# Two of the 16 row-tile transposes of each channel pair go from TensorE to a DMA transpose of two f16 parts

## The chip, the cores and the metric

The kernel runs on one core of one Trainium2 chip. Its time is the device time of one execution in microseconds (us); lower is better. A TensorE column stream, VectorE, ScalarE, GpSimd and SyncE (which here only issues DMAs) run side by side and meet at semaphores.

## What is computed

A residual block over 64 sequences of 128 channels and 2048 positions: a mixing matrix chosen for each sequence, then for each channel a long convolution with a decaying kernel K (a sum of 64 complex exponentials), a direct term, and a mask by length.

```python
x = x + einsum('bct,bcd->bdt', x, weights[condition])           # 64 x 128 x 2048
K = 2 * einsum('hn,hnl->hl', Ct, exp(dtA[:, :, None] * arange(L))).real
y = irfft(rfft(x, 2L) * rfft(K, 2L))[..., :L] + x * D[:, None]   # causal convolution
x = x + y * (arange(L) < length[:, None])
```

## The kernel before, in words

The first part (some 320 us) multiplies each sequence by its matrix plus the identity and stores the result u to a DRAM scratch, channel by channel. Its instructions are L506, L680, L433 and the loads and stores around them. The change doesn't touch it.

The second part walks over 64 pairs of channels (h = 0 and 1 within a pair). The 2048 positions of a channel are cut into 8 pieces of 256; a row tile `u_row` holds 128 rows (2 x 64 sequences) and NG = 4 groups of 256 positions. For every pair:

- TensorE transposes the f32 row tile in 128x128 blocks (`transpose_u`, L518): 16 blocks, k = 0 to 15, where q = k // 4 is (channel, half of 128 positions) and g = k % 4 is the group. The four groups of a q fill one PSUM bank.
- ScalarE turns that bank into the high f16 part of `u_t` (`u_hi`, L694), and VectorE makes the low part, scaled bank less high part (`u_lo`, L958).
- `inputs_to_state` (L532, 12 matmuls of 448 columns) makes what each piece adds to the state, with the table `gt_sb`, which two DMA transposes make (L314).
- `advance` (L544, 6 small matmuls, j = 1 to 6) carries the state from piece to piece. Each j needs the state of the one before in f16: ScalarE `state_hi` (L702), then VectorE `state_lo` (L963).
- `out_part` (L567, L573, L576; k = 0 to 7) makes the outputs from `toep` (a Toeplitz table), `u_t`, `x_t` (a rearranged copy of part of `u_t`, `first_half`, L973) and the states. ScalarE empties the bank (`out_evac`, L710), VectorE lays the unmasked rows of `u_row` over it (`overlay`, L988), and SyncE stores it (L327).
- GpSimd makes the tables of later pairs: `outer` (L409 for the products g_x and g_y, two each, then L413), `outer_lo` (L418) and `make_lambda` (L425).

The order on each engine is written out by hand, slot by slot. In slot c TensorE does `out_part` k = 0, 1 of pair c-1, then `inputs_to_state` of pair c, then k = 2 to 7 of pair c-1 with `advance` 1 to 6 of pair c behind them. The transposes of pair c+1 are put into the `out_part`s, two in each (`between`). VectorE and ScalarE follow tables of steps: "s" state, "u" parts of u_t, "o" output, "t" `fold_toeplitz` (L980), "x" `first_half`, "g" g_hi. VectorE's table is

```python
steps = (("s", c - 1, 7), ("u", c, 3), ("o", c - 2, 3), ("t", c, 0), ("u", c + 1, 0),
         ("o", c - 1, 0), ("s", c, 1), ("x", c, 0), ("s", c, 2), ("x", c, 1), ("s", c, 3), ...
```

All loads, stores and DMA transposes of this part are issued by SyncE, in the order of its `slot`.

Of the kernel before, what the change touches and what calls it, by code (L numbers as in the profile page):

```python
# [38 lines left out]
LENGTHS = 8  # L39
WAVES = 5  # L40
XS = 6
STAGES = 4
# [23 lines left out]
def build(nc, x, cond, length, w_in, log_dt, c_in, log_a, a_im, d_in, out):  # L66
# [6 lines left out]
    with ctx:  # L73
# [15 lines left out]
        ident = sb("ident", [P, P], F32)  # L89
        eyes = sb("eyes", [P, 2, NM], F16)  # L90
        lam_v = sb("lam_v", [P, H, 2, 2], F16)
        mask_i = sb("mask_i", [P, Q], I32)
# [99 lines left out]
        s_gt = [sem(f"s_gt{i}") for i in range(2)]  # L192
        s_st, s_sth, s_stl = (sem(n) for n in ("s_st", "s_sth", "s_stl"))
        s_xt, s_tz = sem("s_xt"), sem("s_tz")
        s_out, s_y, s_ov = (sem(n) for n in ("s_out", "s_y", "s_ov"))
# [41 lines left out]
        def state(t, part, j):  # L237
            return ap(t, part * NG * ROWS + at(j), [[2 * NG * ROWS, 2], [1, NB]])

        def new_state(j):  # L240
# [10 lines left out]
        def _(sp):  # L251
# [59 lines left out]
            def transpose_g(i, c):  # L311

                for lo in (0, NM):
                    sp.dma_start(gt_sb[c % 2][:, :, :, :, lo:lo + NM].rearrange("p h a b m -> p (h a b) m"),  # L314
                                 g_sb[c % 4][NM - lo:P - lo, :, :, :].rearrange("p h a t -> p (h a t)"),
                                 transpose=True).then_inc(s_gt[c % 2], 16)

            def store_out(i, c, h):
                o = 2 * (c % 2) + h
                if (c, h) == (PAIRS - 1, 1):  # L320
                    for v in range(2):
                        store_last(sp, 0, v)
                    return
                sp.wait_ge(s_ov, 4 * (UN * i + c) + 2 * h + 2)
                for j in range(JJ):
                    dst = bass.AP(out.tensor, (2 * (UN * i + c) + h) * T + j * NG * Q, [[H * T, NB], [1, NG * Q]])
                    sp.dma_start(dst, o_sb[o][j * NB:(j + 1) * NB, :, :].rearrange("p g t -> p (g t)"))\  # L327
                        .then_inc(s_store[o], 16)
# [17 lines left out]
            def slot(i, c):  # L346
# [24 lines left out]
                if c == 0:  # L371
                    store_half(NB - 1, 1, EARLY, H, s_last)
                elif c < EARLY // 2 - 2:
                    for n in range(SPLIT_FROM + 2 * c - 2, SPLIT_FROM + 2 * c):
                        store_half(n, 1, EARLY, H, s_kept)
                if has(i, c - 1):
                    store_out(i, c - 1, 0)
# [93 lines left out]
        def _(pe):  # L471
# [38 lines left out]
            def transpose_u(i, c, k):  # L510

                q, g, n = k // NG, k % NG, UN * i + c
                if k % 8 == 0:
                    pe.wait_ge(s_row[c % 4][k // 8], 16 * (i + c // 4 + 1))
                if g == 0:
# [3 lines left out]
                                    u_row[c % 4][:, h, g, tb * P:(tb + 1) * P], ident[:, :])  # L519
                if g == NG - 1:  # L520
                    last.then_inc(s_ut, 1)
# [3 lines left out]
            def inputs_to_state(i, c):  # L525
                n = UN * i + c
                pe.wait_ge(s_gt[c % 2], 32 * (UN // 2 * i + c // 2 + 1))
                pe.wait_ge(s_ul, 4 * n + 4)
                wait(pe, s_stl, 7 * n)
                for h in range(2):  # L530
# [95 lines left out]
        def _(act):  # L626
# [62 lines left out]
            def u_hi(i, c, q):  # L689
                n = UN * i + c  # L690
                act.wait_ge(s_ut, 4 * n + q + 1)
                if q == 0:
                    wait(act, s_out, 4 * (n - 3))
                act.activation(u_t[c % 4][:, q // 2, q % 2, 0, :], bank[:, 4 + q, :], ACT.Copy, scale=US)\  # L694
                    .then_inc(s_uh, 1)

            def state_hi(i, c, j):
# [21 lines left out]
            def slot(i, c):  # L719
                steps = (("s", c - 1, 7), ("u", c, 3), ("o", c - 2, 3), ("g", c + 2, 0), ("u", c + 1, 0),  # L720
                         ("o", c - 1, 0), ("s", c, 1), ("s", c, 2), ("u", c + 1, 1), ("s", c, 3),
                         ("o", c - 1, 1), ("s", c, 4), ("s", c, 5), ("u", c + 1, 2),
                         ("s", c, 6), ("o", c - 1, 2))
                for what, of, k in steps if c else first:
# [5 lines left out]
                    if has(i, of):  # L730
                        if what == "s":
                            state_hi(i, of, k)
                        elif what == "u":
                            u_hi(i, of, k)
                        elif what == "o":
                            out_evac(i, of, k)
                        else:
                            g_hi(i, of)
# [6 lines left out]
        def _(dve):  # L745
# [209 lines left out]
            def u_lo(i, c, q):  # L955
                dve.wait_ge(s_uh, 4 * (UN * i + c) + q + 1)
                t = u_t[c % 4]
                dve.scalar_tensor_tensor(out=t[:, q // 2, q % 2, 1, :], in0=bank[:, 4 + q, :], scalar=US,  # L958
                                         in1=t[:, q // 2, q % 2, 0, :], op0=MUL, op1=SUB).then_inc(s_ul, 1)

# [5 lines left out]
            def first_half(i, c, part):  # L966

                n = UN * i + c
                if part == 0:
                    dve.wait_ge(s_ul, 4 * n + 4)  # L970
                    wait(dve, s_out, 4 * (n - 1))
                to = slice(NM, P) if part == 0 else slice(0, NM)
# [26 lines left out]
            def slot(i, c):  # L999
                steps = (("s", c - 1, 7), ("u", c, 3), ("o", c - 2, 3), ("t", c, 0), ("u", c + 1, 0),  # L1000
                         ("o", c - 1, 0), ("s", c, 1), ("x", c, 0), ("s", c, 2), ("x", c, 1), ("s", c, 3),
                         ("u", c + 1, 1), ("s", c, 4), ("o", c - 1, 1), ("s", c, 5), ("u", c + 1, 2), ("s", c, 6), ("o", c - 1, 2))
                for what, of, k in steps if c else first:
                    if has(i, of):
# [4 lines left out]
                        elif what == "u":  # L1009
                            u_lo(i, of, k)  # L1010
                        elif what == "x":
                            first_half(i, of, k)
# [28 lines left out]
```

## Time and profile before

| | |
|---|---|
| Time, median of 3 runs | 1087.58 us (1077.77 to 1088.26) |
| The profiled execution | 1079.03 us |
| Its span, first to last instruction | 1077.2 us |
| Mean granted TensorE clock | 0.996 |
| Busy: PE, DVE, ACT, POOL | 93%, 72%, 51%, 47% of the span |

The profile names engines PE (TensorE), PEld (its weight loads), DVE (VectorE), ACT (ScalarE), POOL (GpSimd), SP (SyncE; SPq is what it issues to its DMA queue). A row of the timeline is start, duration, engine, line, operation, output<-inputs, shapes, count; in square brackets the idle time ahead of it and who ended it. Matmul rows overlap, since the ends of matmuls are modelled: the distance from one start to the next is what an instruction costs the engine.

### The profile page before, as it was taken

The page shows a single profiled execution, that of the slowest core. Times are in us where ns is not written, and L with a number is a line of the kernel's source. Part 1 is how long each engine was busy: PE and PEld are TensorE (multiplying, and loading weights), DVE is VectorE, ACT ScalarE, POOL GpSimd, SP SyncE. Part 2 cuts the span into 40 slices and gives each one's busy share as a digit, 9 for nine tenths or more (in the row PEclk, how much of TensorE's full clock was granted, in tenths as well). Part 3 has the DMA queues.
Part 4 walks back from the last instruction along what each step waited for, and adds up shares of the span by engine and source line. Part 5 has one row for each costly group of instructions (what it writes and reads, how often), then busy time and mean ns, then how long its engine had stood idle before and what let it go on. Part 6 is the DMA issues. An engine that isn't in the chain of part 4 may idle for free.

```text
span 1077.2 us, 29210 instructions
## 1 busy us (share of the span) xinstructions
PE 1001.6 (93%) x11616; PEld 737.0 (68%) x11616; DVE 770.7 (72%) x1711; ACT 546.6 (51%) x1162; POOL 503.0 (47%) x542
## 2 busy tenths in 40 slices
PE   7977779677898999999999999999999999999998
PEld 4333234222347888888888888888788888888886
DVE  3988950000017888888888888888888888888885
ACT  2643434344444555556555555555555555555543
POOL 2211041200205666666655665665665665666630
PEclk9999999999999999999999999999999999999999
DMA  9999999999999999999999999999999999999994
GB/s 328 423 422 424 422 424 423 377 424 424 424 339 320 265 270 270 232 240 234 217 243 221 223 237 226 233 232 225 223 234 211 227 233 225 225 228 234 231 213 119
DMA packets 171719, 305.48 MB, mean 284 GB/s; under 512 B 80370, under 2 KB 113522, under 8 KB 163394
## 3 DMA queue, kind: packets, MB, share of 16 engines
q1 hardware_dynamic: 171266, 303.16, 99.5%
q8 instruction: 94, 1.54, 0.6%
q14 instruction: 39, 0.32, 0.1%
q0 software_dynamic: 160, 0.20, 0.1%
q10 hardware_dynamic: 160, 0.26, 0.1%
HBM read 152.37 MB, written 134.41 MB: 266 GB/s over the span
## 4 chain that ended last, share of the span: by engine, by line
PE 76%; DMA 17%; ACT 3%; issue 2%; SPq 1%; DVE 1%; ACTq 0%
PE bank L567 16%; DMA u_scratch<-stage 15%; PE bank L576 15%; PE bank L532 13%; PE bank L518 10%; PE bank L506 9%; PE bank L544 7%; PE bank L573 5%; ACT stage L680 2%; DMA x_f<-in_x 1%; DVE x_t L973 1%; DMA u_row<-u_scratch 1%; SPq L314 1%; ACT ring L680 0%; SPq L266 0%
## 5 line engine op out<-in xcount | busy, mean ns | idle before, releaser
L567 PE MATMUL bank<-toep,u_t 128*128 128x192 f16 (+1 forms) x3072 | 342.7, 220 | 0.1
L576 PE MATMUL bank<-g_sb,st_sb 128*128 128x256 f16 x1536 | 305.9, 273 | 0.4 <-issue 0.4
L506 PE MATMUL bank<-x_f,w_buf 128*128 128x512 f32 x512 | 236.7, 608 | 60.4 <-ACT stage L680 43.2
L518 PE MATMUL bank<-ident,u_row 128*128 128x128 f32 x1024 | 277.6, 275 | 2.2 <-issue 1.2
L702 ACT ACTIVATE st_sb<-bank 128x128 f16<-128x128 f32 x448 | 123.8, 276 | 287.8 <-PE bank L544 195.6
L567 PEld LDWEIGHTS bank<-toep,u_t 128*128 128x128 f16 x3072 | 231.4, 98 | 15.2 <-issue 1.4
L506 PEld LDWEIGHTS bank<-x_f,w_buf 128*128 128x128 f32 x512 | 93.8, 192 | 198.0 <-issue 109.7
L988 DVE COPY_PREDICATED o_sb<-mask,u_row 128x512 f32<-128x512 uint8 x256 | 206.1, 805 | 16.5 <-issue 16.5
L958 DVE SCALAR_TENSOR_TENSOR u_t<-bank,u_t 128x512 f16<-128x512 f32 x256 | 176.3, 689 | 37.5 <-ACT u_t L694 35.6
L573 PE MATMUL bank<-toep,x_t 128*128 128x64 f16 x2048 | 188.1, 193 | 0.5 <-issue 0.5
L425 POOL TENSOR_TENSOR lam_sb<-eyes,lam_v 128x512 f16<-128x512 f16 x64 | 75.5, 1180 | 231.7 <-PE bank L544 231.7
L694 ACT ACTIVATE u_t<-bank 128x512 f16<-128x512 f32 x256 | 152.2, 595 | 53.1 <-PE bank L518 48.6
L680 ACT ACTIVATE stage<-bank 128x1024 f32<-128x1024 f32 x100 | 96.8, 1021 | 150.7 <-DMA u_scratch<-stage 119.5
L963 DVE TENSOR_TENSOR st_sb<-bank,st_sb 128x128 f16<-128x128 f32 x448 | 129.8, 290 | 54.6 <-ACT st_sb L702 51.2
L573 PEld LDWEIGHTS bank<-toep,x_t 128*128 128x128 f16 x2048 | 157.5, 98 | 0.6 <-issue 0.6
L532 PE MATMUL bank<-u_t,gt_sb 128*128 128x448 f16 x768 | 155.7, 352 | 1.9 <-DMA gt_sb<-g_sb 1.9
L710 ACT ACTIVATE o_sb<-bank 128x512 f32<-128x512 f32 x256 | 153.3, 599 | 4.1 <-PE bank L576 4.0
L576 PEld LDWEIGHTS bank<-g_sb,st_sb 128*128 128x128 f16 x1536 | 149.3, 98 | 5.8
L518 PEld LDWEIGHTS bank<-ident,u_row 128*128 128x128 f32 x1024 | 143.8, 141 | 10.9 <-issue 1.5
L544 PE MATMUL bank<-st_sb,lam_sb 128*128 128x64 f16 x2304 | 130.1, 192 | 2.9 <-DVE st_sb L963 2.3
L433 POOL TENSOR_TENSOR w_buf<-w_f,ident 128x128 f32<-128x128 f32 x64 | 33.5, 528 | 210.3 <-PE bank L506 205.6
L409 POOL TENSOR_TENSOR g_y<-alpha_im,beta_im 128x256 f32<-128x256 f32 x128 | 129.8, 1033 | 0.0
(130 smaller groups left out, 880.3 us busy)
## 6 DMA issues: line engine op xcount, KB each, us to landing
x_f<-in_x SPq DMA_DIRECT2D x64, 1024.0 KB, 19.6
u_row<-u_scratch SPq DMA_DIRECT2D x128, 512.0 KB, 5.8
out<-o_sb SPq DMA_DIRECT2D x254, 256.0 KB, 3.8
u_scratch<-stage SPq DMA_DIRECT2D x50, 1024.0 KB, 17.7
toep<-k_scratch SPq DMA_DIRECT2D x64, 256.0 KB, 6.0
u_scratch<-ring SPq DMA_DIRECT2D x13, 512.0 KB, 14.6
u_scratch<-kept SPq DMA_DIRECT2D x10, 448.0 KB, 6.9
gt_sb<-g_sb SPq DMA_TRANSPOSE x128, 5.5
```

The lines of the kernel that those rows point to most:

```text
L409: pool.tensor_tensor(out=ap(dst[r], h * Q, [[16, 16], [1, 16]]), in0=ap(ta, o, [[1, 16], [0, 16]]), in1=ap(tb, o, [[0, 16], [1, 16]]), op= ...
L506: last = pe.matmul(bank[:, 4 * (n % 2) + k, :], w_buf[n % XS][:, :], x_f[n % XS][:, k * 512:(k + 1) * 512], start=True, stop=True)
L518: last = pe.transpose(bank[:, 4 + q, g * P:(g + 1) * P], u_row[c % 4][:, h, g, tb * P:(tb + 1) * P], ident[:, :])
L532: last = pe.matmul(bank[:, h, 0:(NJ - 1) * NB], gt_sb[c % 2][:, h, a, 1 - tb, :], u_t[c % 4][:, h, tb, b, 0:(NJ - 1) * NB], start=(m == 0) ...
L544: last = pe.matmul(bank[:, h, at(j):at(j) + NB], lam_sb[c % 2][:, h, a, :, :].rearrange("p k m -> p (k m)"), st_sb[c % 2][:, h, b, at(j):a ...
L567: pe.matmul(bank[:, y, col + tb * P + NM:col + Q], u[:, h, tb, a, rows_], t[:, h, b, NM:Q - tb * P], start=first, stop=False, skip_group_c ...
L573: pe.matmul(bank[:, y, col + tb * P:col + tb * P + NM], x_t[c % 2][:, h, tb, rows_], t[:, h, b, 0:NM], start=False, stop=False, skip_group ...
L576: last = pe.matmul(bank[:, y, col:col + Q], st[:, h, a, gr * ROWS:(gr + 1) * ROWS], g[:, h, b, :], start=False, stop=(m == 2), skip_group_ ...
L694: act.activation(u_t[c % 4][:, q // 2, q % 2, 0, :], bank[:, 4 + q, :], ACT.Copy, scale=US)\
L710: act.activation(o_sb[o][:, 2 * (v % 2):2 * (v % 2) + 2, :].rearrange("p g t -> p (g t)"), bank[:, 2 + v % 2, :], ACT.Copy, scale=1.0 / (U ...
L958: dve.scalar_tensor_tensor(out=t[:, q // 2, q % 2, 1, :], in0=bank[:, 4 + q, :], scalar=US, in1=t[:, q // 2, q % 2, 0, :], op0=MUL, op1=SU ...
L988: dve.copy_predicated(o_sb[2 * (c % 2) + v // 2][:, g2, :].rearrange("p g (b t) -> p (g b) t", t=P), mask[:, g2, :].rearrange("p g (b t) - ...
```

## The change

From the fourth pair on (`TURNED = 3`), for channel h = 0 of each pair (`TH = 1`), the last of the four groups of rows (g = 3) isn't transposed by TensorE. ScalarE makes the high f16 part of those 256 columns straight from the row tile (`parts_hi`), VectorE the low part (`parts_lo`), both into a new buffer `parts` with one copy, and one DMA transpose of 128 x 512 f16 elements writes both into `u_t` (`transpose_parts`). So TensorE does 14 transposes a pair in place of 16, over 61 pairs 122 less. `u_hi` and `u_lo` of q = 0 and 1 handle 384 columns in place of 512.

```diff
+        parts = sb("parts", [P, TH, 2, 2, P], F16)
+        def groups(c, h):
+            return NG - 1 if c >= TURNED and h < TH else NG
...
+            def transpose_parts(c):
+                sp.wait_ge(s_pl, c - TURNED + 1)
+                wait(sp, s_out, 4 * (c - 3))
+                sp.dma_start(ap(u_t[c % 4], (NG - 1) * ROWS, [[NG * ROWS, TH * 4], [1, ROWS]]),
+                             parts[:, :, :, :, :].rearrange("p h b a t -> p (h b a t)"), transpose=True)\
+                    .then_inc(s_pt, 16)
...
+                if TURNED <= c + 1 < PAIRS:
+                    transpose_parts(c + 1)
                 if has(i, c - 1):
                     store_out(i, c - 1, 0)
...
                 q, g, n = k // NG, k % NG, UN * i + c
+                if g >= groups(c, q // 2):
+                    return
...
                 pe.wait_ge(s_ul, 4 * n + 4)
+                wait(pe, s_pt, 16 * (n - TURNED + 1))
...
+            def parts_hi(c):
+                for h in range(TH):
+                    act.wait_ge(s_row[c % 4][h], 16 * (c // 4 + 1))
+                wait(act, s_pt, 16 * (c - TURNED))
+                act.activation(parts[:, :, :, 0, :],
+                               u_row[c % 4][:, 0:TH, NG - 1, :].rearrange("p h (b t) -> p h b t", t=P),
+                               ACT.Copy, scale=US).then_inc(s_ph, 1)
...
-                         ("o", c - 1, 0), ("s", c, 1), ("s", c, 2), ("u", c + 1, 1), ("s", c, 3),
+                         ("o", c - 1, 0), ("p", c + 1, 0), ("s", c, 1), ("s", c, 2), ("u", c + 1, 1), ("s", c, 3),
...
+                cols = groups(c, q // 2) * ROWS
+                dve.scalar_tensor_tensor(out=t[:, q // 2, q % 2, 1, 0:cols], in0=bank[:, 4 + q, 0:cols], scalar=US,
+                                         in1=t[:, q // 2, q % 2, 0, 0:cols], op0=MUL, op1=SUB).then_inc(s_ul, 1)
+            def parts_lo(c):
+                dve.wait_ge(s_ph, c - TURNED + 1)
+                dve.scalar_tensor_tensor(out=parts[:, :, :, 1, :],
+                                         in0=u_row[c % 4][:, 0:TH, NG - 1, :].rearrange("p h (b t) -> p h b t", t=P),
+                                         scalar=US, in1=parts[:, :, :, 0, :], op0=MUL, op1=SUB).then_inc(s_pl, 1)
...
                     dve.wait_ge(s_ul, 4 * n + 4)
+                    wait(dve, s_pt, 16 * (n - TURNED + 1))
...
-                         ("o", c - 1, 0), ("s", c, 1), ("x", c, 0), ("s", c, 2), ("x", c, 1), ("s", c, 3),
+                         ("o", c - 1, 0), ("p", c + 1, 0), ("s", c, 1), ("x", c, 0), ("s", c, 2), ("x", c, 1), ("s", c, 3),
```

On VectorE, in every slot, from `fold_toeplitz` to the second state. Before:

```order
L980 COPY toep<-toep 64x4x64 [waits s_t3]
L958 SCALAR_TENSOR_TENSOR u_t<-bank,u_t 128x512 [waits s_uh]
L986 MEMSET pad 1x1 [waits s_y]
L988 COPY_PREDICATED o_sb<-mask,u_row 128x512
L963 TENSOR_TENSOR st_sb<-bank,st_sb 128x2x64 [waits s_sth]
L973 COPY x_t<-u_t 64x2048 [waits s_out,s_ul]
L963 TENSOR_TENSOR st_sb<-bank,st_sb 128x2x64 [waits s_sth]
```

And in the changed kernel, where line numbers are larger:

```order
L1022 COPY toep<-toep 64x4x64 [waits s_t3]
L993 SCALAR_TENSOR_TENSOR u_t<-bank,u_t 128x384 [waits s_uh]
L1028 MEMSET pad 1x1 [waits s_y]
L1030 COPY_PREDICATED o_sb<-mask,u_row 128x512
L998 SCALAR_TENSOR_TENSOR parts<-u_row,parts 128x2x128 [waits s_ph]
L1004 TENSOR_TENSOR st_sb<-bank,st_sb 128x2x64 [waits s_sth]
L1015 COPY x_t<-u_t 64x2048 [waits s_out,s_pt,s_ul]
L1004 TENSOR_TENSOR st_sb<-bank,st_sb 128x2x64 [waits s_sth]
```

The new instruction stands between the overlay and the first state of the pair; the copy behind that state has a wait for the DMA transpose more.

On SyncE, one slot. Before:

```order
L314 DMA_TRANSPOSE gt_sb<-g_sb 128x8x64 [waits s_st,s_g]
L314 DMA_TRANSPOSE gt_sb<-g_sb 128x8x64
L327 DMA out<-o_sb 64x1024 [waits s_ov]
L327 DMA out<-o_sb 64x1024
L301 DMA u_row<-u_scratch 128x1024 [waits s_ov]
L308 DMA toep<-k_scratch 128x4x256 [waits s_out]
L327 DMA out<-o_sb 64x1024 [waits s_ov]
```

Changed:

```order
L323 DMA_TRANSPOSE gt_sb<-g_sb 128x8x64 [waits s_st,s_g]
L323 DMA_TRANSPOSE gt_sb<-g_sb 128x8x64
L343 DMA out<-o_sb 64x1024 [waits s_ov]
L343 DMA out<-o_sb 64x1024
L310 DMA u_row<-u_scratch 128x1024 [waits s_ov]
L317 DMA toep<-k_scratch 128x4x256 [waits s_out]
L330 DMA_TRANSPOSE u_t<-parts 128x4x128 [waits s_out,s_pl]
L343 DMA out<-o_sb 64x1024 [waits s_ov]
```

The new transpose is issued behind the `toep` load and ahead of the next output store.

## Rows read from the trace of the kernel before

**Rows 1.** Busy us of PE, PEld, DVE, ACT, POOL, then clock, DMA share, GB/s

```profile
700.00:800.00 100.00, 99.14 (x1464) 84.22 (x1462) 86.97 (x191) 55.98 (x140) 61.60 (x59) 1.00 1.04 228
```

**Rows 2.** Waits from 500 to 1000 us: total, times, longest

```profile
PE bank L544 <- DVE st_sb L963: 1.9, 4, 0.8
```

**Rows 3.** TensorE's timeline: transposes inside out_part, and one pair

```profile
706.94 0.27 PE L518 MATMUL bank<-ident,u_row 128*128 128x128 f32 x1
707.04 0.33 PE L567 MATMUL bank<-toep,u_t 128*128 128x192 f16 x2
...
707.85 2.43 PE L532 MATMUL bank<-u_t,gt_sb 128*128 128x448 f16 x12
...
711.17 0.34 PE L544 MATMUL bank<-st_sb,lam_sb 128*128 128x64 f16 x6
...
713.55 0.33 PE L544 MATMUL bank<-st_sb,lam_sb 128*128 128x64 f16 x6
...
719.47 2.43 PE L532 MATMUL bank<-u_t,gt_sb 128*128 128x448 f16 x12
```

**Rows 4.** VectorE's timeline in the same pair

```profile
707.39 0.73 DVE L988 COPY_PREDICATED o_sb<-mask,u_row 128x512 f32<-128x512 uint8 x1
...
708.15 1.03 DVE L980 COPY toep<-toep 64x256 f16<-64x256 f16 x1
709.22 0.69 DVE L958 SCALAR_TENSOR_TENSOR u_t<-bank,u_t 128x512 f16<-128x512 f32 x1
709.83 1.02 DVE L988 COPY_PREDICATED o_sb<-mask,u_row 128x512 f32<-128x512 uint8 x1
...
710.75 0.27 DVE L963 TENSOR_TENSOR st_sb<-bank,st_sb 128x128 f16<-128x128 f32 x1
711.05 0.80 DVE L973 COPY x_t<-u_t 64x2048 f16<-64x2048 f16 x1
711.88 0.29 DVE L963 TENSOR_TENSOR st_sb<-bank,st_sb 128x128 f16<-128x128 f32 x1
712.20 0.69 DVE L973 COPY x_t<-u_t 64x2048 f16<-64x2048 f16 x1
```

**Rows 5.** GpSimd's timeline in the same pair

```profile
707.82 1.28 POOL L418 TENSOR_TENSOR g_sb<-g_x,g_sb 128x512 f16<-128x512 f32 x1 [0.62 <-ACT g_sb L651]
709.07 1.19 POOL L409 TENSOR_TENSOR g_x<-alpha_re,beta_re 128x256 f32<-128x256 f32 x2
710.22 2.10 POOL L409 TENSOR_TENSOR g_y<-alpha_im,beta_im 128x256 f32<-128x256 f32 x2
712.41 1.62 POOL L413 TENSOR_TENSOR g_x<-g_x,g_y 128x512 f32<-128x512 f32 x1
```

**Rows 6.** VectorE in the last pair, when GpSimd has ended

```profile
1057.53 0.22 DVE L980 COPY toep<-toep 64x256 f16<-64x256 f16 x1
```

**Rows 7.** The pair from 765.32 us: VectorE, GpSimd, TensorE, and its window

```profile
769.91 1.80 DVE L973 COPY x_t<-u_t 64x2048 f16<-64x2048 f16 x1
...
769.88 1.28 POOL L413 TENSOR_TENSOR g_x<-g_x,g_y 128x512 f32<-128x512 f32 x1
...
772.18 0.34 PE L544 MATMUL bank<-st_sb,lam_sb 128*128 128x64 f16 x6 [0.76 <-DVE st_sb L963]
...
765.32:778.00 12.68, 11.82 (x170) 9.83 (x168) 11.22 (x23) 6.48 (x17) 7.03 (x8) 1.00 0.96 214
```

**Rows 8.** VectorE by line and shape (count, busy, mean ns); ScalarE's timeline

```profile
L755 DVE SCALAR_TENSOR_TENSOR ex<-ex 128x256 f32<-128x256 f32 x8 | 3.5, 443 | 0.3
...
710.32 0.28 ACT L702 ACTIVATE st_sb<-bank 128x128 f16<-128x128 f32 x1 [1.40 <-PE bank L532]
```

**Rows 9.** SyncE's queue in the pair, and transposes' issue to landing, 440 to 1050 us

```profile
711.85 0.43 SPq L308 DMA_DIRECT2D toep<-k_scratch  x1
715.21 1.12 SPq L327 DMA_DIRECT2D out<-o_sb  x2
...
DMA to landing us min/median/max: 3.2/5.5/7.9
```

More of the change, by code:

```diff
@@ L40 @@
 WAVES = 5
+TURNED = 3
+TH = 1
 XS = 6
@@ L193, in build @@
         s_st, s_sth, s_stl = (sem(n) for n in ("s_st", "s_sth", "s_stl"))
+        s_ph, s_pl, s_pt = (sem(n) for n in ("s_ph", "s_pl", "s_pt"))
         s_xt, s_tz = sem("s_xt"), sem("s_tz")
@@ L519, in transpose_u @@
                                     u_row[c % 4][:, h, g, tb * P:(tb + 1) * P], ident[:, :])
-                if g == NG - 1:
+                if g == groups(c, h) - 1:
                     last.then_inc(s_ut, 1)
@@ L693, in u_hi @@
                     wait(act, s_out, 4 * (n - 3))
-                act.activation(u_t[c % 4][:, q // 2, q % 2, 0, :], bank[:, 4 + q, :], ACT.Copy, scale=US)\
+                cols = groups(c, q // 2) * ROWS
+                act.activation(u_t[c % 4][:, q // 2, q % 2, 0, 0:cols], bank[:, 4 + q, 0:cols], ACT.Copy, scale=US)\
                     .then_inc(s_uh, 1)
+            def parts_hi(c):
[5 more added lines that the diff above has]
+                               ACT.Copy, scale=US).then_inc(s_ph, 1)
             def state_hi(i, c, j):
@@ L734, in slot @@
                             u_hi(i, of, k)
+                        elif what == "p":
+                            if of >= TURNED:
+                                parts_hi(of)
                         elif what == "o":
@@ L957, in u_lo @@
                 t = u_t[c % 4]
-                dve.scalar_tensor_tensor(out=t[:, q // 2, q % 2, 1, :], in0=bank[:, 4 + q, :], scalar=US,
-                                         in1=t[:, q // 2, q % 2, 0, :], op0=MUL, op1=SUB).then_inc(s_ul, 1)
+                cols = groups(c, q // 2) * ROWS
+                dve.scalar_tensor_tensor(out=t[:, q // 2, q % 2, 1, 0:cols], in0=bank[:, 4 + q, 0:cols], scalar=US,
[5 more added lines that the diff above has]
+                                         scalar=US, in1=parts[:, :, :, 0, :], op0=MUL, op1=SUB).then_inc(s_pl, 1)
             def state_lo(i, c, j):
@@ L1010, in slot @@
                             u_lo(i, of, k)
+                        elif what == "p":
+                            if of >= TURNED:
+                                parts_lo(of)
                         elif what == "x":
```

## The prediction

> **What bounds the kernel now.** I read first the busy time by stretches. In the second part TensorE is busy 99% of the time at a granted clock of 1.00, VectorE 87% [rows 1]; the chain of waits of the page gives nearly all of this part to TensorE too. So a column less on TensorE should be time won, and the list of waits seems to agree: TensorE's wait for VectorE adds up to 1.9 us in 500 us [rows 2]. But that list shows only gaps above some tenths, and 87% is not much room for an engine whose instructions come in a fixed order. So I then laid the timelines of one pair side by side.
>
> One pair is the distance between two `inputs_to_state`: 719.47 - 707.85 = 11.62 us [rows 3]. Over the 52 pairs from 441.89 us to 1045.81 it is 11.42 at the least, 11.52 in the median and 11.61 in the mean. VectorE has no pause from 707.39 to about 712.9 [rows 4]: overlay, `fold_toeplitz`, `u_lo`, overlay, and only then the first state, which TensorE's first `advance` needs. That state ends at 711.02 and the `advance` starts at 711.17 [rows 3, 4]. From the end of the matmuls ahead of it, counted by their columns, to this `advance` there are 0.06 us in half of the pairs and 0.01 in the others; there are 0.15 us at the least from a state to its `advance`. So at this one place VectorE ends last already, or within a tenth of it.
>
> The timelines show a second thing. VectorE's `fold_toeplitz` takes 1.03 us while GpSimd's L418 runs, and ends with it; with GpSimd idle it takes 0.22 [rows 4 to 6]. So the two engines take turns at something. The overlay takes 1.02 beside GpSimd's L409 and 0.73 at 707.39. `u_lo`, which reads PSUM and one tile of SBUF, takes its 0.69 beside L409 as elsewhere. And who gets the turn is to be seen: L418 had been waiting since 707.82 behind the overlay of 707.39, and it came ahead of `fold_toeplitz`, which was VectorE's very next instruction [rows 4, 5]. The other way round, the overlay of 709.83 came in between two L409 of GpSimd. Whoever waits gets the next turn.
>
> The Trainium skill, "SBUF — State Buffer", section "Who interferes with whom", says the same of the kinds: two SBUF inputs, or a copy in a two-port mode, contend with GpSimd, one PSUM input and one SBUF input does not. It goes further than the rows in one point, that the pair of ports is held for the whole instruction. The trace has turns pass earlier: an L409 alone takes 0.60 (half of 1.19), the first g_y ends at 711.27 (710.22 + half of 2.10), so it began at 710.67, some 0.18 before the overlay's recorded end at 710.85 [rows 4, 5]. By the page's rule each handover below would come at least 0.12 later, two of them in each of 61 pairs, 15 us more, 1167 in place of 1152; I go by the rows.
>
> **The change part by part.** Times are in the clock of the pair of 707.85.
>
> TensorE loses 2 transposes a pair. One costs 707.04 - 706.94 = 0.11 us from start to start [rows 3]; 122 of them are 13.1 us. They stand in `out_part` 1 and 3. The first gain falls ahead of the `advance` that waits for VectorE, and the second just behind it, so both are worth something only if VectorE keeps up.
>
> ScalarE's `parts_hi` (256 columns, between 0.28 for 128 and 0.60 for 512) falls into the 1.40 us for which ScalarE stands idle ahead of its first state [rows 8]: nothing.
>
> VectorE's `u_lo` of q = 0 loses 128 columns: (0.69 - 0.29)/384 us each, 0.13 us [rows 4]. But the overlay behind it is waiting for GpSimd's two g_x, which end at 710.26 [rows 5], so that gain is lost there: 0.
>
> VectorE's `parts_lo` is the new step, directly behind the overlay and ahead of the first state. Its nearest row is a scalar_tensor_tensor of 256 f32 columns out of SBUF, 0.44 us [rows 8]; at the lowest it is the 0.42 of a line through 0.29 and 0.69. It has two SBUF inputs, so it takes turns with GpSimd. GpSimd's first g_y has waited since the overlay began, so by what L418 did it goes first and ends at 710.22 + 1.05 = 711.27 [rows 5]; VectorE's copy, issued at 711.05, took 0.80 in place of 0.69 for it, so its turn came at 711.16 [rows 4]. `parts_lo` then runs from 711.16 to 711.60. The first state goes from 711.02 to about 711.85, and the `advance` from 711.17 to 712.00: **+0.83**.
>
> What is late next: GpSimd's second g_y gets its turn at about 711.48 and runs 0.6, to 712.09. The copy `first_half` 0 (issued 711.88) follows to 712.66. L413 is waiting by then and gets the next turn at about 712.5, for 1.28, to 713.80. The second state is ready 0.71 behind the `advance` (711.88 - 711.17) and ends at 712.98, and the copy `first_half` 1 is issued at 713.01: behind L413 now, where before it was ahead (712.20 against 712.41). The trace of before has this very case, by chance, in the pair from 765.32: L413 at 769.88, the copy at 769.91 took 1.80 us and ended 0.55 after L413, TensorE waited 0.76, and the pair took 12.68 us, though the clock stayed 1.00 [rows 7]. Here the copy ends at 713.80 + 0.55 = 714.35, the third state at 714.67, and the third `advance` starts at 714.82 in place of 713.55 [rows 3]: **+1.27**. From there on TensorE sets the pace again, some 1.2 a step (713.55 - 711.17 for two).
>
> The chain into this starts with the last `advance` of the pair before, through ScalarE, so it is the same in each pair and the delay is paid once per pair. 61 pairs by 1.27 are 77.5 us. Some 4 to 5 us of it are there already (the pair of 765.32 and a few smaller ones like it), which leaves +73.
>
> SyncE: the new issue comes after `toep` (712.28), `parts_lo` is ready by then, and SyncE would next wait for an overlay until 715.21 [rows 9], so an issue of 1 to 3 us is hidden. The transpose should land as those of `gt_sb` do, 3.2 to 7.9 us after issue, so at 720.2 at the latest; `inputs_to_state` then comes at 719.47 + 1.27 = 720.7. No cost, with half a microsecond to spare in the worst case.
>
> Sum: 1079.03 + 73 = **1152 us**. The profiled execution is among the short ones; the median is 8.5 us above it, and if those 8 us are pairs like that of 765.32 they are part of the 73 already, so I don't add them.
>
> **The rivals.** (a) VectorE keeps its turn: `parts_lo` starts at once at 710.87 and GpSimd waits. Then the first state is late by 0.42 to 0.53, GpSimd moves back with it, and the second copy stays ahead of L413; the third state is late by some 0.3 to 0.5. 61 by 0.4 is +25: **1104**. Against it speaks L418 ahead of `fold_toeplitz`, in every pair. (b) TensorE gets its columns back: VectorE's chain has room after all, because the 0.13 us off `u_lo` and a short `parts_lo` cancel. It decides below an added 0.1 us between overlay and first state, and then the 13.1 us are won: **1066**, faster. For it speak only the 99% of TensorE; against it the gap of 0.06 in half the pairs. (c) The DMA transpose is late. From 8.4 us after issue on, `inputs_to_state` waits; at 10 us that is 1.6 more a pair, **1250**. For it speaks that it stands behind two loads in the queue, against it the 7.9 us. (d) Only part of `parts_lo` shows, +0.15 a pair: **1088**.
>
> **How the numbers follow.** Forecast 0.64, (a) 0.17, (c) 0.06, (b) 0.05, (d) and what else lies near the old time 0.08. The range of 8 in 10 takes in the forecast and (a): from 1097 (61 by 0.3) to 1172 (the page's rule for the handovers, and 5 us for a landing that is sometimes late). A measurement of this kernel can tell about 1% from no change. Faster by more than that: 0.05; within it: 0.06; slower: 0.89.
>
> **What would show it.** Right: a pair of about 12.7 us; `parts_lo` with 0.7 to 0.9 us instead of 0.44; TensorE waiting for VectorE's state about 1.0 us at the first `advance` and 0.5 at the third; the second copy of `first_half` at 1.3 us or more in nearly all pairs; L413 at 1.3 and less. Wrong: `parts_lo` at 0.44 and a pair of 11.9 (rival a), a wait of TensorE for the DMA at L532's successor (rival c), no wait of TensorE and 11.3 us (rival b).

## The result, and the profile after

The changed kernel takes **1149.71 us** (median of 4 runs, 1149.0 to 1150.51); the kernel before had 1085.94 beside it (median of 4). The ratio is **1.0591, with an interval of 1.0559 to 1.0624**. The profiled execution took 1149.0 us, its span is 1146.8, against 1079.03 and 1077.2: +69.6 us of span.

The busy time of the same stretch of the second part, as in [rows 1]:

```profile
700.00:800.00 100.00, 91.43 (x1321) 74.77 (x1320) 88.29 (x181) 51.14 (x135) 53.77 (x54) 1.00 0.98 217
```

TensorE falls from 99.14 to 91.43 us of 100 with the clock at 1.00; VectorE rises only from 86.97 to 88.29. No engine is full: two of them wait for each other. The chain of the page puts 34% of the span on PE and 30% on DVE. The waits from 500 to 1100 us say where, as in [rows 2] (total, times, longest):

```profile
PE bank L565 <- DVE st_sb L1004: 48.6, 93, 1.0
```

That is 93 waits in 47 pairs, two in each, where before there were four in all. The timelines of one pair show both. TensorE, as in [rows 3]:

```profile
735.37 2.43 PE L553 MATMUL bank<-u_t,gt_sb 128*128 128x448 f16 x12
...
739.56 0.33 PE L565 MATMUL bank<-st_sb,lam_sb 128*128 128x64 f16 x6 [0.76 <-DVE st_sb L1004]
...
742.39 0.34 PE L565 MATMUL bank<-st_sb,lam_sb 128*128 128x64 f16 x6 [0.35 <-DVE st_sb L1004]
...
748.05 0.73 PE L553 MATMUL bank<-u_t,gt_sb 128*128 128x448 f16 x3
```

VectorE, as in [rows 4]:

```profile
736.85 0.56 DVE L993 SCALAR_TENSOR_TENSOR u_t<-bank,u_t 128x384 f16<-128x384 f32 x1
737.33 1.16 DVE L1030 COPY_PREDICATED o_sb<-mask,u_row 128x512 f32<-128x512 uint8 x1
...
738.39 0.82 DVE L998 SCALAR_TENSOR_TENSOR parts<-u_row,parts 128x256 f16<-128x256 f32 x1
739.14 0.28 DVE L1004 TENSOR_TENSOR st_sb<-bank,st_sb 128x128 f16<-128x128 f32 x1
739.45 0.80 DVE L1015 COPY x_t<-u_t 64x2048 f16<-64x2048 f16 x1
740.27 0.29 DVE L1004 TENSOR_TENSOR st_sb<-bank,st_sb 128x128 f16<-128x128 f32 x1
740.60 1.32 DVE L1015 COPY x_t<-u_t 64x2048 f16<-64x2048 f16 x1
741.95 0.29 DVE L1004 TENSOR_TENSOR st_sb<-bank,st_sb 128x128 f16<-128x128 f32 x1
```

GpSimd, as in [rows 5]:

```profile
737.85 1.84 POOL L427 TENSOR_TENSOR g_y<-alpha_im,beta_im 128x256 f32<-128x256 f32 x2
739.77 1.60 POOL L431 TENSOR_TENSOR g_x<-g_x,g_y 128x512 f32<-128x512 f32 x1
```

The pair takes 748.05 - 735.37 = 12.68 us. `parts_lo` takes 0.82 beside g_y, the first state is late by it, GpSimd's product sum (L431, once L413) is at its door at 739.77 and goes ahead of the second `first_half` copy of 740.60, which ends 0.55 after it (741.92 against 741.37), and the third `advance` waits a second time.

The new buffer, by name (durations in ns, minimum, median, maximum; then who waited, us and times; then the landing):

```profile
L998 DVE SCALAR_TENSOR_TENSOR parts<-u_row,parts x61: 406/826/831, 353.1 to 1117.1; 128x256 f16<-128x256 f32 x61
L330 SPq DMA_TRANSPOSE u_t<-parts x61: 1208/1217/3247, 355.7 to 1117.6; - x61
...
  PE bank L553: 2.5, 2
...
DMA to landing us min/median/max: 3.8/5.5/8.2
```

The minimum of 406 ns is from the end of the kernel, where GpSimd has no product left to make. There the pair from 1104.07 us needs 11.48 us (the same pair before: 11.60), with the whole change in it, TensorE busy for 11.45 of them and the DMAs at 242 GB/s:

```profile
1106.03 0.73 DVE L1030 COPY_PREDICATED o_sb<-mask,u_row 128x512 f32<-128x512 uint8 x1
...
1106.65 0.41 DVE L998 SCALAR_TENSOR_TENSOR parts<-u_row,parts 128x256 f16<-128x256 f32 x1
...
1108.42 0.69 DVE L1015 COPY x_t<-u_t 64x2048 f16<-64x2048 f16 x1
```

So the trace of the changed kernel holds its own control: without GpSimd's g_x, g_y and product sum beside it, the same instruction sequence loses nothing.

**Where the 69.6 us are.** From the starts of `inputs_to_state` in both traces: pairs 2 to 11 take 118.8 us in place of 103.9 (+14.9), pairs 11 to 61 take 635.1 in place of 580.8 (+54.3, median of a pair 12.68 against 11.52), and the rest is the same within half a microsecond. The granted clock explains little of it: in the early pairs it is 0.97, against 1.00 before, of 43.85 busy us some 1.3.

```profile
350.00:400.00 50.00, 43.85 (x601) 35.27 (x599) 41.54 (x84) 23.19 (x62) 25.60 (x27) 0.97 1.02 262
```

The table gives medians over these late pairs, the `advance`s counted from `inputs_to_state`; it serves the experiments too. The last two columns are each from one profiled execution.

| kernel | time, us | ratio [interval] | pair | 1st, 3rd `advance` | pairs 2 to 11 | 11 to 61 |
|---|---|---|---|---|---|---|
| before | 1085.94 | 1 | 11.52 | 3.32, 5.71 | 103.9 | 580.8 |
| after | 1149.71 | 1.059 [1.056, 1.062] | 12.68 | 4.19, 7.02 | 118.8 | 635.1 |
| e1 parts alone | 1147.16 | 1.061 [1.059, 1.063] | 12.68 | 4.07, 6.90 | 115.8 | 634.0 |
| e2 one SBUF input | 1138.0 | 1.052 [1.050, 1.054] | 12.49 | 3.76, 6.83 | 116.3 | 625.0 |
| e3 GpSimd waits | 1123.91 | 1.038 [1.037, 1.040] | 12.17 | 4.19, 6.50 | 113.9 | 615.1 |
| e4 no low part | 1104.11 | 1.022 [1.017, 1.028] | 11.52 | 3.45, 5.75 | 114.0 | 591.7 |
| e5 no low, DMAs | 1085.1 | 1.003 [1.002, 1.005] | 11.42 | 3.45, 5.75 | 113.6 | 576.3 |
| e6 DMA alone | 1107.3 | 1.021 [1.016, 1.026] | 11.87 | 3.33, 5.73 | 113.1 | 601.0 |
| e7 placed later | 1091.36 | 1.009 [1.007, 1.012] | 11.46 | 3.43, 5.75 | 111.7 | 581.7 |
| e8 before, GpSimd waits | 1079.53 | 0.999 [0.997, 1.001] | 11.49 | 3.32, 5.70 | 105.1 | 577.6 |
| e9 e7, fold moved | 1093.57 | 1.010 [1.007, 1.013] | 11.50 | 3.27, 5.75 | 112.3 | 584.9 |
| e10 all | 1092.2 | 1.009 [1.005, 1.012] | 11.70 | 3.27, 5.75 | 106.3 | 591.0 |
| e11 before, fold moved | 1084.05 | 1.001 [0.999, 1.003] | 11.59 | 3.42, 5.81 | 105.7 | 582.1 |
| e12 no low, ahead | 1143.69 | 1.058 [1.053, 1.063] | 12.54 | 3.91, 6.84 | 117.3 | 627.9 |

Ratios are against the kernel before in the same round of runs: 1081.82 for e1 to e4, 1080.57 for e5 to e8, 1083.61 for e9 to e12.

### The profile page after: what moved, and what is told of

Read it like the earlier page. It is cut to its first block, busy times and chain, and to the rows that moved or that the text cites. A ratio compares the mean times of both kernels' runs of the same rounds, so it can differ in the third digit from the quotient of the medians.

```text
span 1146.8 us, 29330 instructions
## 1 busy us (share of the span) xinstructions
PE 1011.3 (88%) x11494; PEld 723.0 (63%) x11494; DVE 841.7 (73%) x1772; ACT 549.0 (48%) x1223; POOL 485.6 (42%) x542
## 4 chain that ended last, share of the span: by engine, by line
PE 34%; DVE 30%; DMA 17%; issue 12%; ACT 6%; SPq 1%; DVEq 0%; ACTq 0%
DMA u_scratch<-stage 14%; DVE x_t L1015 10%; PE bank L524 8%; PE bank L588 6%; DVE u_t L993 6%; PE bank L597 6%; PE bank L565 5%; DVE toep L1022 5%; PE bank L538 4%; DVE st_sb L1004 4%; DVE parts L998 4%; ACT u_t L716 3%; PE bank L594 2%; ACT stage L701 2%; PE bank L553 2%
## 5 line engine op out<-in xcount | busy, mean ns | idle before, releaser
L597 PE MATMUL bank<-g_sb,st_sb 128*128 128x256 f16 x1536 | 293.5, 273 | 1.0 <-issue 1.0
L538 PE MATMUL bank<-ident,u_row 128*128 128x128 f32 x902 | 244.6, 275 | 0.8 <-DMA u_row<-u_scratch 0.7
L1030 DVE COPY_PREDICATED o_sb<-mask,u_row 128x512 f32<-128x512 uint8 x256 | 213.9, 836 | 17.4 <-issue 17.4
L524 PEld LDWEIGHTS bank<-x_f,w_buf 128*128 128x128 f32 x512 | 94.6, 193 | 195.8 <-issue 113.1
L993 DVE SCALAR_TENSOR_TENSOR u_t<-bank,u_t 128x512 f16<-128x512 f32 (+1 forms) x256 | 160.0, 625 | 38.2 <-ACT u_t L716 36.2
L565 PEld LDWEIGHTS bank<-st_sb,lam_sb 128*128 128x128 f16 x2304 | 104.2, 97 | 110.9 <-issue 102.5
L701 ACT ACTIVATE stage<-bank 128x1024 f32<-128x1024 f32 x100 | 96.8, 1021 | 149.7 <-DMA u_scratch<-stage 118.8
L716 ACT ACTIVATE u_t<-bank 128x512 f16<-128x512 f32 (+1 forms) x256 | 139.9, 546 | 13.6 <-PE bank L538 13.3
L597 PEld LDWEIGHTS bank<-g_sb,st_sb 128*128 128x128 f16 x1536 | 141.1, 98 | 7.7 <-issue 1.6
L1015 DVE COPY x_t<-u_t 64x2048 f16<-64x2048 f16 x128 | 133.0, 1039 | 4.0
L538 PEld LDWEIGHTS bank<-ident,u_row 128*128 128x128 f32 x902 | 126.6, 142 | 10.4 <-issue 2.0
```

Source lines behind the costliest of these rows:

```text
L524: last = pe.matmul(bank[:, 4 * (n % 2) + k, :], w_buf[n % XS][:, :], x_f[n % XS][:, k * 512:(k + 1) * 512], start=True, stop=True)
L538: last = pe.transpose(bank[:, 4 + q, g * P:(g + 1) * P], u_row[c % 4][:, h, g, tb * P:(tb + 1) * P], ident[:, :])
L565: last = pe.matmul(bank[:, h, at(j):at(j) + NB], lam_sb[c % 2][:, h, a, :, :].rearrange("p k m -> p (k m)"), st_sb[c % 2][:, h, b, at(j):a ...
L597: last = pe.matmul(bank[:, y, col:col + Q], st[:, h, a, gr * ROWS:(gr + 1) * ROWS], g[:, h, b, :], start=False, stop=(m == 2), skip_group_ ...
L716: act.activation(u_t[c % 4][:, q // 2, q % 2, 0, 0:cols], bank[:, 4 + q, 0:cols], ACT.Copy, scale=US)\
L993: dve.scalar_tensor_tensor(out=t[:, q // 2, q % 2, 1, 0:cols], in0=bank[:, 4 + q, 0:cols], scalar=US, in1=t[:, q // 2, q % 2, 0, 0:cols], ...
```

## The experiments

**e1: the two parts alone.** All 16 transposes stay on TensorE, and there is no DMA transpose; `parts_hi` and `parts_lo` are still made.

```diff
-            return NG - 1 if c >= TURNED and h < TH else NG
+            return NG
...
-                if TURNED <= c + 1 < PAIRS:
-                    transpose_parts(c + 1)
...
-                wait(act, s_pt, 16 * (c - TURNED))
+                wait(act, s_pl, c - TURNED)
```

> The changed kernel with only its new ScalarE and VectorE instructions kept: TensorE does all 16 transposes again, there is no DMA transpose of parts and no wait for one. My theory (VectorE's parts_lo and the turns it takes with GpSimd cost everything): a pair of 12.7 us and 1150 us, as the changed kernel. Rival (the DMA transpose, its issue or the wait for it costs the time): 1079 to 1090.

Measured: 1147.16 us, a ratio within the interval of the whole change. Two element-wise instructions of together 1.24 us a pair are the whole loss; by the traces the DMA transpose and the two transposes less make pairs 2 to 11 longer by 3.0 us and pairs 11 to 61 by 1.1. In this kernel the queue and the columns hardly matter. The pair takes 12.68 us either way, since in both kernels TensorE waits for VectorE.

**e2: one SBUF input.** The low part is subtracted from a PSUM bank of the same size in place of `parts` (other numbers, same work), so that only one of its inputs is in SBUF.

```diff
-                                         scalar=US, in1=parts[:, :, :, 0, :], op0=MUL, op1=SUB).then_inc(s_pl, 1)
+                                         scalar=US, in1=bank[:, 7:8, 0:Q].rearrange("p h (b t) -> p h b t", t=P), op0=MUL, op1=SUB).then_inc(s_pl, 1)
```

> The changed kernel, but parts_lo takes its second input from PSUM (bank 7, 256 columns) in place of the high part in SBUF, so the low part holds other numbers. Place, columns and waits are the same. My theory (two SBUF inputs make it wait for GpSimd's turn): parts_lo takes 0.41 to 0.45 us in place of 0.82, the first advance comes 0.4 us sooner; GpSimd's second g_y and L431 then come sooner too, so that the second copy of first_half still comes behind L431: a pair of about 12.4, 1133 us (1105 if the copy comes ahead of it). Rival (it is slow by its shape or by what ScalarE does beside it): 0.82 and 1150.

```profile
L998 DVE SCALAR_TENSOR_TENSOR parts<-u_row,bank x61: 393/400/410, 352.8 to 1104.4; 128x256 f16<-128x256 f32 x61
...
720.08 1.04 DVE L1015 COPY x_t<-u_t 64x2048 f16<-64x2048 f16 x1
...
720.65 1.60 POOL L431 TENSOR_TENSOR g_x<-g_x,g_y 128x512 f32<-128x512 f32 x1
...
721.47 1.32 DVE L1015 COPY x_t<-u_t 64x2048 f16<-64x2048 f16 x1
```

0.40 in place of 0.83 us: the other half was waiting for GpSimd, and the kind of the inputs decides that, as [rows 4] had it for `u_lo`. The first `advance` comes 0.43 earlier. But the kernel takes 1138.0, only 9 us less than e1 in the same round, since the third `advance` comes 0.19 earlier and no more. `parts_lo` takes no turn here, so GpSimd isn't moved back by it: its product sum starts 4.21 us into the pair (4.56 before, medians), the first copy takes 1.04 in place of 0.80, since it starts while the second g_y runs, and the second copy is still behind the product sum. The delay of the first state and the lost turn of the copy are two costs.

**e3: GpSimd waits.** The product sum of the changed kernel waits until both copies are made.

```diff
                 pool.wait_ge(s_gx, 4 * n + 4)
+                wait(pool, s_xt, 2 * (n - 2))
```

> The changed kernel with one wait more: GpSimd starts the subtraction L431 only when both copies of first_half of the running pair are done. My theory: parts_lo still takes 0.82, but the second copy takes 0.69 in place of 1.32, the third advance comes 0.55 us sooner, a pair of 12.1, 1117 us. Rival (the second copy's lateness is hidden, parts_lo alone sets the pair): 1147 to 1150.

```profile
POOL g_x L432 <- DVE x_t L1016: 83.2, 47, 2.6
...
PE bank L566 <- DVE st_sb L1005: 31.0, 43, 1.0
```

TensorE's waits go from 93 to 43 in some 49 pairs, about one a pair. The third `advance` comes at 6.50, only a step behind the second; the first one stays at 4.19. The pair takes 12.17: of the 1.16 us that the change costs a pair, **0.51 is GpSimd's turn ahead of the copy, and 0.65 the late first state**. GpSimd waits 1.8 us a pair for it, and TensorE shows no wait for GpSimd. The kernel takes 1123.91, 7 us more than expected; its late pairs contain seven pauses of TensorE of another kind, 6.2 us in all, to which the last section comes.

**e4: no low part.** `parts_lo` is a memset of one element; the low part is zero. Everything else of the change is there.

```diff
-                dve.scalar_tensor_tensor(out=parts[:, :, :, 1, :],
...
+                dve.memset(parts[0:1, 0, 0, 1, 0:1], 0.0).then_inc(s_pl, 1)
```

> The changed kernel without the low part's computation: parts_lo is a memset of one element, so the low half of parts stays zero. TensorE's 122 transposes stay away, the DMA transpose and ScalarE's part stay. My theory (VectorE's chain to the first state is the bound even before the change, so that little of TensorE's 13 us comes back): 1075 us (1072 to 1079). Rival (TensorE's columns were the bound): 1066. Rival (the DMA transpose costs): above 1085.

Measured: 1104.11. My theory and the first rival, which both had a gain, missed; the second rival, that the DMA transpose costs, is what happened. The median pair is that of before, 11.52 us. In addition TensorE pauses for about a microsecond in every fourth pair (13.2 us in 14 pauses of the late pairs: 12 put down to "issue", and 2 in which it waits for the transposed parts to land), and pairs 2 to 11 cost 10 us. TensorE's waits for the parts over the whole kernel (us, times):

```profile
  PE bank L553: 6.6, 4
```

So the DMA transpose is not free, and with the shorter pair it sometimes lands too late.

**e5: neither low part nor DMAs.** As e4, and the DMA transpose is issued for the first four pairs only; later pairs use what lies in `u_t`.

```diff
-                if TURNED <= c + 1 < PAIRS:
+                if TURNED <= c + 1 < TURNED + 4:
                     transpose_parts(c + 1)
...
-                wait(pe, s_pt, 16 * (n - TURNED + 1))
+                wait(pe, s_pt, 16 * min(n - TURNED + 1, 4))
```

> The kernel e4_no_low, with the DMA transpose left out too from the fifth of its pairs on: u_t keeps in those columns what the first four wrote. So TensorE's 122 transposes are away and nearly nothing stands in their place. If the 20 to 25 us that e4 lies above my 1075 come from the DMA transpose (its late landings and pauses in which TensorE waits for nothing the profile shows): pairs of 11.4 us as in e4 and few pauses, 1070 us. If they come from the shorter pairs alone: 1100 again.

Measured: 1085.1, between the two expected values. Without the DMAs nearly all of the pauses are gone (11 to 61: 15.4 us less than e4, 4.5 less than before; of the twelve "issue" pauses two are left). These 4.5 us are what two transposes less give in the late pairs, where their columns would be 50 x 2 x 0.11 = 11. The early pairs stay 9.7 us longer, with only four DMA transposes. The rest of that isn't explained, but 5.3 us of it are a plain wait (348 to 440 us):

```profile
PE bank L553 <- DMA u_t<-parts: 5.3, 2, 3.0
```

**e6: the DMA alone.** As e4, but TensorE does all 16 transposes, and the DMA writes to a buffer that nobody reads. `parts_hi` on ScalarE, the one-element memset and the waits for the DMA stay.

```diff
-                sp.dma_start(ap(u_t[c % 4], (NG - 1) * ROWS, [[NG * ROWS, TH * 4], [1, ROWS]]),
+                sp.dma_start(turned[:, :, :],
```

> The kernel before with the DMA transpose alone: TensorE does all 16 transposes, the new DMA transpose writes a buffer that nobody reads, TensorE and VectorE wait for it as in the changed kernel, parts_lo is a memset of one element. If the transpose costs by itself: pairs of 11.5 in the median, but more pairs with a pause, 1095 to 1100. If it is free: 1080 to 1083.

1107.3 (1097.59 to 1108.87), more than expected: 61 DMA transposes of 128 KB beside a kernel that is otherwise nearly unchanged cost **27 us** between medians, 17 to 28 by the interval of the ratio. `parts_hi` and the memset have no share in it in the late pairs: e5 has them there too, without the DMAs, and is no slower than before. TensorE's waits from 500 to 1050 us:

```profile
PE bank L598 <- issue: 5.6, 4, 2.7
PE bank L566 <- DVE st_sb L1003: 4.7, 12, 0.8
...
PE bank L566 <- issue: 2.7, 2, 1.9
PE bank L589 <- issue: 2.7, 5, 0.8
PE bank L595 <- issue: 2.1, 3, 1.2
```

"Issue" means that the profile shows nothing that TensorE waited for. The section at the end says what it was.

**e7: placed later.** The whole change, made one pair further ahead and with both steps moved behind the states that were late: on ScalarE behind the second state, on VectorE behind `u_t` part 1.

```diff
-                         ("o", c - 1, 0), ("p", c + 1, 0), ("s", c, 1), ("s", c, 2), ("u", c + 1, 1), ("s", c, 3),
+                         ("o", c - 1, 0), ("s", c, 1), ("s", c, 2), ("p", c + 2, 0), ("u", c + 1, 1), ("s", c, 3),
...
-                         ("o", c - 1, 0), ("p", c + 1, 0), ("s", c, 1), ("x", c, 0), ("s", c, 2), ("x", c, 1), ("s", c, 3),
-                         ("u", c + 1, 1),
+                         ("o", c - 1, 0), ("s", c, 1), ("x", c, 0), ("s", c, 2), ("x", c, 1), ("s", c, 3),
+                         ("u", c + 1, 1), ("p", c + 2, 0),
...
-                    transpose_parts(c + 1)
+                    transpose_parts(c + 2)
```

> The whole change, with its steps one pair further ahead and elsewhere: in slot c ScalarE makes the high part of pair c+2 behind state 2, VectorE the low part behind u_lo of q = 1 (behind GpSimd's L431), SyncE issues the transpose for pair c+2. My theory (the place in VectorE's order cost some 70 us, and the DMA transpose some 20): the 1.2 us a pair are gone, 1095 to 1105 us. If the DMA's cost were only its late landings, which a whole pair more of time removes: 1075 to 1080.

```profile
L998 DVE SCALAR_TENSOR_TENSOR parts<-u_row,parts x61: 415/635/644, 348.5 to 1052.8; 128x256 f16<-128x256 f32 x61
...
DMA to landing us min/median/max: 2.4/4.6/8.3
```

1091.36 in place of 1149.71, below the expected 1095 to 1105: the ratio falls from 1.059 to 1.009. **Five sixths of the loss hung on the place of two steps**, though VectorE still does the same work. e7 also gives the DMA a pair more to land, but that isn't what it gains by: e1, without the DMA, has the whole loss. The late pairs now cost 0.9 us in all against before; the 8 us of the early pairs remain.

**e8: the kernel before, GpSimd waits.** The line of e3 alone, put into the kernel before.

> The kernel before with e3's wait: GpSimd starts L413 only when both copies of first_half are done. If pairs like that of 765.32 are collisions of L413 with the second copy: none of them is left, 3 to 5 us less than the kernel before. If the order of the two follows from a delay elsewhere: no change.

1079.53, 0.999 [0.997, 1.001]. The chance collisions like that of [rows 7] are gone (no pause of TensorE for VectorE in 50 pairs) and 11 to 61 is 3.2 us shorter by the traces, less than the runs can tell.

**e9, e10, e11: `fold_toeplitz` moved.** Three attempts at a version that beats the kernel before. e9 is e7 with `fold_toeplitz` behind the overlay in VectorE's steps; e10 adds the wait of e3 and begins with pair 10; e11 is the kernel before with the step moved and the wait. The step, as e11 moves it:

```diff
-                steps = (("s", c - 1, 7), ("u", c, 3), ("o", c - 2, 3), ("t", c, 0), ("u", c + 1, 0),
-                         ("o", c - 1, 0), ("s", c, 1), ("x", c, 0), ("s", c, 2), ("x", c, 1), ("s", c, 3),
+                steps = (("s", c - 1, 7), ("u", c, 3), ("o", c - 2, 3), ("u", c + 1, 0),
+                         ("o", c - 1, 0), ("t", c, 0), ("s", c, 1), ("x", c, 0), ("s", c, 2), ("x", c, 1), ("s", c, 3),
```

> The kernel e7_placed_later with VectorE's fold_toeplitz moved behind the overlay, directly ahead of the first state, so that it no longer holds up u_lo and the overlay while GpSimd has its turn with L436. If VectorE's chain to the first state is what keeps TensorE's two removed transposes from paying: the gap of 0.18 us ahead of the first advance is gone, pairs of 11.2 us in place of 11.42, 10 to 12 us less than e7, 1079 to 1082. If fold_toeplitz is only held up later by GpSimd's L427 and the first state with it: no gain or a loss, 1091 to 1110.

> The kernel e9_fold_moved, with the change beginning at the pair with number 10, behind the late stores of the kept halves, and with e3's wait of GpSimd. If the slow pairs 3 to 9 (8 to 11 us in e4 to e7) come from the DMA transposes beside those stores: another 8 us less, with the wait 3 more, 1068 to 1072, 1% below the kernel before. If they come from elsewhere: as e9.

> The kernel before with the two additions of e10 that have nothing to do with the change: fold_toeplitz behind the overlay, and GpSimd's wait. TensorE has all its columns here and is the bound within 0.06 us: 1075 to 1079, 2 to 5 us less than before.

All three missed the gain that was hoped for: 1093.57, 1092.2 and 1084.05. In e9 the first `advance` comes 0.16 earlier than in e7 (3.27), and the second doesn't (4.58): the first copy takes 1.01 in place of 0.79 (medians), so nothing is won. In e10 the early pairs cost 5.4 us less than in e7, as meant, but the product sum, now held until the second copy has ended, meets `parts_lo`:

```profile
721.09 1.28 POOL L432 TENSOR_TENSOR g_x<-g_x,g_y 128x512 f32<-128x512 f32 x1 [0.71 <-DVE x_t L1016]
...
721.72 0.93 DVE L999 SCALAR_TENSOR_TENSOR parts<-u_row,parts 128x256 f16<-128x256 f32 x1
...
722.57 0.28 DVE L1005 TENSOR_TENSOR st_sb<-bank,st_sb 128x128 f16<-128x128 f32 x1
```

0.93 in place of 0.64, and the fourth state is late (fourth `advance` at 7.20, in e9 at 6.93): the collision had only moved. None of the versions tried beats the kernel before.

**e12: no low part, one pair ahead.** As e4, with both steps at the same places but for pair c + 2, so that the DMA has a pair more to land. It was to tell a late landing from a disturbance of other transfers.

> The kernel e4_no_low with everything of the transpose one pair further ahead, issued at the same point of the slot. If the 15 us that e4 loses against e5 over 50 pairs are late landings for which TensorE waits, they are gone: 1090. If the transpose costs by being in the queue there, beside the loads: 1104 again.

1143.69, far from both. It told neither, since it built a wait of its own:

```profile
ACT parts L724 <- DMA u_row<-u_scratch: 96.5, 47, 3.9
```

`parts_hi` stands ahead of ScalarE's first state, and at that place the half of row tile c + 2 that it reads (channel h = 0) is only just landing; ScalarE waits for it 2.05 us a pair (96.5 / 47; it is idle 1.40 there before [rows 8]), and the state, the `advance` and the copy's turn wait behind it. e7 has the same step two states later, and there it is 5 us in all. So e12 doesn't settle what e4's pauses are; by e4's own trace 2.0 of their 13.2 us are waits for a landing.

## Why the prediction was right, and where not

Forecast 1152, measured 1149.71; the forecast case (GpSimd's g_y first, then the product sum ahead of the second copy) is the one that happened, and e1, e2, e3 and e7 show its steps one by one. Point by point:

- **VectorE's chain is the bound that the busy shares hide** (0.06 us of room ahead of the first `advance`): right, and e7 shows it with the work unchanged.
- **`parts_lo` from the handover to +0.44**: right. Counted from the last `advance` of the pair before, the first `advance` comes at 2.14 + 4.19 = 6.33 against 2.25 + 3.32 = 5.57: +0.76 for +0.83. e2 shows that half of the instruction's time is the wait for GpSimd. (The first g_y can't have waited "since the overlay began", as the prediction has it: the g_x ahead of it ends at 710.26, in the middle of the overlay [rows 4, 5]. It is next in line all the same.)
- **The copy behind the product sum, third `advance` +1.27**: right in order and nearly in size, 9.16 against 7.96, **+1.20**. The copy ends 0.55 after the product sum, as taken over from [rows 7], and the pair takes that group's 12.68. TensorE's waits are shown as 0.76 and 0.35, for my 1.0 and 0.5. L431 takes 1.60, where I had 1.3 and less: it is at the door while the first copy still runs. e3 takes this turn away, and 0.51 us with it.
- **The Trainium skill's rule on the port pair.** In the pair above the overlay ends at 738.49; one g_y of 0.60 [rows 5] and `parts_lo` of 0.41 one after the other would end at 739.50, but `parts_lo` ends at 739.21. So the turns pass before the recorded ends in this trace too; whether a record ends after the pair is free isn't shown. The Trainium skill ("SBUF — State Buffer", "Who interferes with whom") has the pair held for the whole instruction, by which the forecast was 1167; the handovers in the recorded times don't agree with that, and e2 agrees with its rule on kinds (0.40 us in place of 0.83).
- **Rival (a)** fell with the 0.82 us. Its price, 25 us, wasn't tried. e2 is near to it, `parts_lo` at once and 0.40 long, and costs 56 us; but in e2 `parts_lo` takes no turn from GpSimd, and rival (a) has GpSimd moved back by it, which was its reason for the copy to stay ahead of the product sum. What e2 shows is that a delay of the state alone, with GpSimd not moved back, loses that place.
- **The transposes are worth nothing**: right in this kernel. `inputs_to_state` starts 0.11 earlier (2.14 behind the last `advance`, 2.25 before), but the first `advance` doesn't: it comes at 6.33, and in e1, with all 16 transposes, at 2.25 + 4.07 = 6.32, and the pair is 12.68 in both. Where VectorE is less late they are worth something, 4.5 us over 50 pairs in e5.
- **SyncE and the DMA cost nothing**: the step that failed, though the sum hardly shows it. The prediction looked at the issue and the landing only. In the changed kernel the issue is hidden and the landing is in time in the late pairs (8.2 at the most for 7.9). But e6 has 27 us for the DMAs where TensorE is the bound, 20 us of it in the late pairs, where 13.8 us are fifteen pauses that are neither a wait for the issue nor one for the landing (last section). In the changed kernel TensorE waits for VectorE 1.0 us a pair anyway (48.6 us in 47 pairs), and there little of it shows (after against e1: 4 us by the traces, transposes included). What is left is in the early pairs: they were to cost 9 x 1.27 = 11.4 and cost 14.9.
- **The sum came out better than its terms, and that is luck.** 50 late pairs by 1.27, less 4 to 5, would be 59; they cost 54.3. The last two pairs, 2.5 in the sum, lose nothing, since GpSimd's products are done by then. The early pairs cost 3.5 more than forecast. So the +73 of the sum met +70 in the profiled executions. Between the medians it is 1149.71 - 1085.94 = 63.8; that the sum stood on the short profiled execution of before brought the total nearer.

## What to carry to other kernels

Where an engine with a fixed order feeds a recurrence, ask of a new instruction first what stands right behind it, and what other engine gets a turn at the shared resource because of the delay: here the same instruction cost 1.2 us a pair in one place and next to nothing in another. A gain of columns on an engine that is 99% busy has to be priced at the next bound, and that was 0.1 us away. Work that is moved to the DMA must be tried alone in the unchanged kernel; beside a larger stall its cost doesn't show.

## What the runs showed of the hardware that was not expected

**TensorE runs out of instructions, and with the new DMA transpose more often.** The pauses put down to "issue" have a visible cause. In e6, TensorE stops at 603.6 us and resumes at 606.25, in the middle of an `out_part`, and the profile shows nothing that it waited for:

```profile
603.37 0.22 PE L595 MATMUL bank<-toep,x_t 128*128 128x64 f16 x2
606.25 0.27 PE L598 MATMUL bank<-g_sb,st_sb 128*128 128x256 f16 x1 [2.66 <-issue]
```

The transfers from 603.8 to 604.8 us contain one packet of the instruction queue (packets, MB, share):

```profile
q8 instruction: 1, 0.02, 6.2%
```

It is 16 KB, began at 603.82 and took 0.99 us. Between two packets of this queue the trace has 255 instructions of TensorE in the mean. In the records of all fourteen kernels from 440 us on, TensorE has 67 "issue" pauses of 0.3 us and more, and two things hold for every one of them:

- **It ends 1.22 to 1.66 us after the end of a packet of this queue.** The packets come some 9 us apart, so a moment chosen at random falls into that strip one time in twenty.
- **It stands at the same place in the program.** Count TensorE's recorded instructions (matmuls, weight loads and its own few semaphore instructions) from the first on: each of the 67 pauses comes 193 to 195 instructions past a multiple of 256.

So TensorE stops at the end of a block of 256 instructions, and goes on when the next packet has come. That is as near as the traces get to showing a wait for instructions. The late packets are those that begin 6.5 to 10.5 us into a pair, behind the issue of the DMA transposes (in e6 all 15 begin 2.5 to 5.5 us after the new one was issued). Of the packets there, in pairs 11 to 61, 3 of 28 came too late before, 0 of 20 in e1, 12 of 32 in e4, 15 of 33 in e6, 2 of 28 in e5; of 543 packets elsewhere in the pair, in all fourteen kernels, none. So one more DMA transpose a pair makes more packets late (e6 against before, e4 against e5); what holds a packet back (the queue, the transposes' packets) wasn't tried. It explains what "issue" hid, and why e3, e4 and e6 lose more than their late waits add up to. The changed kernel and e1, with 12.68 us a pair, have 3 and 0 such pauses. A guess is that a longer pair asks for instructions more slowly; it isn't shown, and e12 has 6 at 12.54 us.

**A turn at the shared resource goes to whoever waits, instruction by instruction**, and so the length of one small VectorE instruction depends on its place: the low part took 0.41 us with GpSimd idle, 0.40 with one PSUM input, 0.64 behind `u_lo` in e7, 0.83 behind the overlay, 0.93 in e10, where the product sum starts just ahead of it.
